# The first hidden units of the MLP move from the last attention step to behind its last values' product

## The chip, the cores and the metric

The kernel runs on one core of one Trainium2 chip. The metric is the device time in microseconds (us) of one execution. The engines are named as the profile names them: PE (TensorE, matrix products), PEld (its weight loads), DVE (VectorE), ACT (ScalarE), POOL (GpSimd) and SP (SyncE, which here only issues transfers). Each engine works through its own list of instructions in order, and the lists meet only at semaphores.

## The reference

Eight sequences of 256 tokens with 512 features are taken through a small non-local attention block (1x1 convolutions, no softmax, batch norm), and then through a transformer block with two cross attentions over the same context (16 heads of 128, one bias key and value added to each head) and an MLP:

```
x = x + attention(layer_norm(x), ctx, weights 1)      # softmax(q k^T / sqrt(128)) v, 16 heads
x = x + attention(layer_norm(x), ctx, weights 2)
h = layer_norm(x)
x = x + gelu(h @ w_fc1 + b_fc1) @ w_fc2 + b_fc2        # 512 -> 2048 -> 512, exact gelu
```

All is float32. The kernel gets that precision by splitting each operand of a product into a high part (rounded to the fp32r format) and the remainder, and by three matrix products in place of one: high by high, high by low, low by high. These three are lines 848, 849 and 850.

## The kernel before

The 2048 rows of x lie in the on-chip memory as 16 tiles of 128 rows, four tiles to a chunk, and there are four chunks (c = 0 to 3). An attention **step** s is one pair of heads for one chunk; there are 64 steps (2 layers x 8 pairs x 4 chunks), numbered 0 to 63. A step has four **items** (two batches x two heads), so the items run from 0 to 255, and the last step, 63, holds items 252 to 255. The work on one item J is:

- `L`, `logits(J)`: PE multiplies queries by keys into the bank `S` (6 matmuls of 258 columns). There is one `S`, so `L` of J+1 waits until ACT has read `S` of J (`exped`).
- DVE takes the minimum of each row (line 1543, `nm`), ACT the exponentials with their sums (line 1225, two of them), DVE the reciprocals of the sums (line 1547), ACT divides by them (line 1233, two).
- `T`, `turn(J)`: PE turns the probabilities (4 small matmuls, line 995) into the bank `T`; ACT copies the high part (line 1243, `PT`), DVE makes the low part (line 1551).
- `P`, `weighted(J)`: PE multiplies by the values into the bank `O` (6 matmuls of 256 columns). ACT reads the high part out (line 1249, `oT`), DVE the low part (line 1558). There is one `O`, so the next `P` waits for that (`o_done`).

What remains goes through a ring of four banks called `U`; a unit takes the bank of the unit four places before it in PE's order and waits until that one has been read out. The units are:

- `q` (s, h): queries of the next step, 12 matmuls, issued in two halves of 6, before and behind a `P`.
- `w` (s, t), t = 0 to 3: output projection of step s for tile t, 6 matmuls, added to x by DVE (line 1535).
- `Z` (n, c, ch), ch = 0 to 3: four small matmuls (line 938) that turn normalised rows. ACT reads them in two dependent instructions (lines 1192 and 1195), DVE in one (line 1515). Norm 2 is the MLP's. Its chunk 1 is turned during step 63, its chunks 2 and 3 behind it.
- `f` (m, i), i = 0 or 1: half of a hidden step of the MLP, 12 matmuls. ACT applies gelu (line 1211, `tmp`) and copies the high part (line 1219), DVE makes the low part `gT` (line 1526, two operands in SBUF).
- `W` (m, t): the second product of the MLP, 6 matmuls, added to x by DVE. There are 32 steps m, chunk m mod 4.

The order of PE is written out by hand: `front_order()`, then `slot_order(s, j)` for the four slots j of each of the 64 steps (one slot an item), then `last_order()`. In a slot, PE does `L` of item J+1, `T` of item J, a first filler, `P` of item J-1 and a second filler; for j = 0 and 2 the fillers are the two halves of a unit `q` of the next step. In the last step there is no next step: the helper `projection` puts there the units `f` (0, 0) and `f` (0, 1), the MLP's first for chunk 0. In slots 1 and 3, and in slots 1 to 3 for `Z`, the fillers are units `w` and `Z`.

ACT and DVE have loops of their own over the same slots. ACT's slot is: queries or hidden (slots 1 and 3), the copy of T (J), the exponentials (J+1), in slots 2 and 3 a `Z` row, `oT` (J-1), the division (J+1), and in slots 1 and 3 one more `Z` row. `hidden(0, j // 2)` stands first in slots 1 and 3 of the last step. DVE's slot has hidden in the same place, between an output and the low part of `PT`. Behind the slots both follow `last_order()`.

`last_order()` starts with P (255), f (1, 0), w (63, 2), w (63, 3), f (1, 1); then Z (2, 2, 0 to 3) mixed with W (0, 0 to 3), f (2, 0), f (2, 1), and Z (2, 3, ...) mixed with W (1, ...); from there on it is regular. DVE does statistics and moments of chunk 3 right behind w (63, 3). POOL splits the MLP's first output weights (`outputs(16)`: a cast at line 644, a subtraction at line 647) once w (63, 3) has been made, then takes a power for chunk 3 once DVE has the moments, then splits the weights `wqs_c` (`queries(17)`) and later adds a bias to the rows. SP's transfers wait for these splits.

Of the kernel before, what the change touches and what calls it, by code (L numbers as in the profile page):

```python
# [38 lines left out]
P = 128  # L39
# [13 lines left out]
STEPS = HBODIES * CHUNKS  # L53
MSTEPS = MBODIES * CHUNKS
ITEMS = 4 * STEPS
# [121 lines left out]
def norm_at(s):  # L177

    for n in range(NORMS):
        c = s - 2 - (n * BODIES * CHUNKS - CHUNKS)  # L180
        if 0 <= c < CHUNKS:
            return n, c
    return None


def projection(s, h, half):
    return ("q", s, h, half) if s < STEPS else ("f", s - STEPS, h, half)


def slot_order(s, j):  # L190

    item = 4 * s + j
    if j in (0, 2):
        first, second = ([projection(s + 1, j // 2, half)] for half in range(2))
    elif j == 1:
        first, second = ([("w", s - 1, t)] if s else [] for t in (2, 3))
    else:
        first, second = ([("w", s, t)] for t in (0, 1))
    rows = [("Z", *norm_at(s), ch) for ch in range(CH)] if norm_at(s) else None
    out = [("L", item + 1)] if item + 1 < ITEMS else []  # L200
    out += [("T", item)] + first
    if rows and j in (1, 3):
        out.append(rows[0 if j == 1 else 3])
    out += [("P", item - 1)] if item else []
    out += second
    if rows and j in (1, 2):
        out.append(rows[j])
    return out


def last_order():

    def f(m, i):
        return [("f", m, i, half) for half in range(2)] if m < MSTEPS else []

    def rows(c):
        return [("Z", LAYERS, c, ch) for ch in range(CH)]

    def mixed(m, c, before):

        out = []
        for t in range(4):
            out += [rows(c)[ch] for ch in before[t]] + [("W", m, t)]
        return out

    out = [("P", ITEMS - 1)] + f(1, 0) + [("w", STEPS - 1, 2), ("w", STEPS - 1, 3)] + f(1, 1)
    out += mixed(0, 2, ((0,), (1,), (2,), (3,))) + f(2, 0) + f(2, 1) + mixed(1, 3, ((), (0, 1), (2,), (3,)))
    for m in range(2, MSTEPS):
        out += f(m + 1, 0) + f(m + 1, 1) + [("W", m, t) for t in range(4)]
    return out  # L230
# [37 lines left out]
def bass_xattn(nc, x_in, ctx_in, thw, thb, pgw, pgb, www, bncol, wa, wk, wv, wb, hcol, vrow,  # L268
               lncol, f1col, orow, out):
    ctx = ExitStack()  # L270
    with ctx:
# [6 lines left out]
        def f(ap):  # L278

            return ap.bitcast(F32)  # L280
# [118 lines left out]
        def bank(*name):  # L399
            return U[:, UNIT[name] % RING, :]  # L400
# [680 lines left out]
        def _(act):  # L1081
# [100 lines left out]
            def rows(n, c, ch):  # L1182
                k = (n * CHUNKS + c) * CH + ch
                act.wait_ge(unit, UNIT["Z", n, c, ch] + 1)
                if k > 1:
                    former = [u for u in UNIT if u[0] == "Z"][k - 2]
                    act.wait_ge(free, FREE[former] + 1)
                else:
                    act.wait_ge(z_x, TILES)
                    act.wait_ge(summed, SUMS)  # L1190
                col = n * CH + ch
                act.activation(hT[c][:, 0, ch, :], bank("Z", n, c, ch), ACT.Identity, bias=lnc[:, 1, col:col + 1],  # L1192
                               scale=lnc[:, 0, col:col + 1]).then_inc(ln_hi, 1)
                act.wait_ge(ln_hi, k + 1)
                act.activation(aff[:, k % 2, :], f(hT[c][:, 0, ch, :]), ACT.Identity, bias=lnn[:, col:col + 1]).then_inc(ln_affine, 1)

            def queries(s, h):
                at_ = 2 * (s // CHUNKS) + h
                act.wait_ge(unit, UNIT["q", s, h] + 1)
                if s and h == 0:  # L1200
                    act.wait_ge(logit, 4 * s - 1)
                elif s:
                    act.wait_ge(logit, 4 * s)
                act.activation(qT[:, 0, h, :], bank("q", s, h), ACT.Identity, bias=hc[:, 0, at_:at_ + 1]).then_inc(hi, 1)

            def hidden(m, i):
                at_ = 2 * (m // CHUNKS) + i
                act.wait_ge(unit, UNIT["f", m, i] + 1)
                if m:
                    act.wait_ge(free, FREE["f", m - 1, i] + 1)  # L1210
                act.activation(tmp[:, i, :], bank("f", m, i), ACT.Gelu, bias=f1c[:, at_:at_ + 1]).then_inc(gelu, 1)  # L1211
                if m > 1 and i == 0:
                    act.wait_ge(unit, UNIT["W", m - 2, 3] + 1)
                elif m == 0 and i == 0:
                    act.wait_ge(logit, ITEMS - 4)
                elif m == 1 and i == 0:
                    act.wait_ge(pv, ITEMS - 4)
                act.wait_ge(gelu, GELU["f", m, i] + 1)
                act.activation(gT[m % 2][:, 0, i, :], tmp[:, i, :], ACT.Copy).then_inc(g_hi, 1)  # L1219

            def exponentials(J):
                r = J % 2
                act.wait_ge(least, J + 1)
                for qt in range(2):
                    ins = act.activation(probs[:, r, qt, 0:257], S[:, qt, 0:257], ACT.Exp, bias=nm[:, r, qt:qt + 1],  # L1225
                                         scale=-1.0, accum_out=sums[:, r, qt:qt + 1])
                ins.then_inc(exped, 1)
# [8 lines left out]
            def turned_hi(J):  # L1236
                act.wait_ge(turned, J + 1)
                if J > 1:
                    act.wait_ge(pv, J - 1)
                else:  # L1240
                    for i in range(4):
                        act.wait_ge(sent[i], 16 * len(KV) // 4)
                act.activation(PT[:, J % 2, 0, :], T[:], ACT.Copy).then_inc(pt_hi, 1)  # L1243
# [35 lines left out]
            for s, j in SLOTS:  # L1279
                J = 4 * s + j  # L1280
                if j % 2 and s + 1 < STEPS:
                    queries(s + 1, j // 2)
                elif j % 2:
                    hidden(0, j // 2)
                turned_hi(J)
                if J + 1 < ITEMS:
                    exponentials(J + 1)
                z_of = norm_at(s)
                if z_of and j > 1:
                    rows(*z_of, j - 1)  # L1290
                if J:
                    weighted_hi(J - 1)
                if J + 1 < ITEMS:
                    divided(J + 1)
                if z_of and j in (1, 3):
                    rows(*z_of, 0 if j == 1 else 3)
# [11 lines left out]
        def _(dve):  # L1308
# [215 lines left out]
            def hidden(m, i):  # L1524
                dve.wait_ge(g_hi, GELU["f", m, i] + 1)
                dve.tensor_tensor(gT[m % 2][:, 1, i, :], tmp[:, i, :], f(gT[m % 2][:, 0, i, :]), ALU.subtract).then_inc(free, 1)  # L1526
# [14 lines left out]
            def least_of(J):  # L1541
                dve.wait_ge(logit, J + 1)
                dve.tensor_reduce(nm[:, J % 2, :], S[:, :, 0:257], AX.X, ALU.min).then_inc(least, 1)  # L1543
# [17 lines left out]
            for k, (what, *a) in enumerate(FRONT):  # L1561
# [10 lines left out]
                elif what == "V":  # L1572
                    r, q, product_of = a
# [23 lines left out]
            for s, j in SLOTS:  # L1597
                J = 4 * s + j
                z_of, z_former, measured = norm_at(s), norm_at(s - 1), norm_at(s + 1) if s else None
                if J + 1 < ITEMS:  # L1600
                    least_of(J + 1)
                if j == 0 and s:
                    if z_former:
                        rows(*z_former, 3)
                    output("w", s - 1, 1)
                elif j == 2:
                    if z_of:
                        rows(*z_of, 0)
                    if s:
                        output("w", s - 1, 3)  # L1610
                if j % 2 and s + 1 < STEPS:
                    queries(s + 1, j // 2)
                elif j % 2:
                    hidden(0, j // 2)
                turned_lo(J)
                if j == 1 and s:
                    output("w", s - 1, 2)
                elif j == 3 and not z_of:
                    output("w", s, 0)
                if J + 1 < ITEMS:  # L1620
                    inverted(J + 1)
                if z_of and j > 1:
                    rows(*z_of, j - 1)
                if J:
                    weighted_lo(J - 1)
                if z_of and j == 3:
                    output("w", s, 0)
                if measured and s > 1:
                    for t in ((0, 1), (2,), (3,), ())[j]:
                        stats_of(s - 1, t)  # L1630
                    if j == 2:
                        moments(*measured)
# [77 lines left out]
```

## Time and profile before

| | |
|---|---|
| median of 3 runs | 2297.21 us (2295.78 to 2297.26) |
| the profiled execution | 2296.15 us |
| its span, first to last instruction | 2294.3 us |
| PE busy | 2271.1 us, 99% of the span |
| DVE busy | 1372.1 us, 60% |
| POOL busy | 1244.9 us, 54% |
| ACT busy | 1168.1 us, 51% |
| mean granted clock of PE | 0.999 |

A profile shows one execution. Its 2294.3 us of span have 1.85 us around them that no engine's instructions fill. PE is busy in nearly every slice of the page; the end of a matmul is modelled, so short idle times are best measured from start to start.

### The profile page before, as it was taken

The numbers are of one execution on the slowest core, as the hardware profiler recorded it, in microseconds if no ns is written. First come the engines' busy times: TensorE is split into PE (matmuls) and PEld (weight loads), VectorE is DVE, ScalarE is ACT, GpSimd is POOL, SyncE is SP. The second block draws the span as 40 slices with busy tenths as digits, with TensorE's granted clock in tenths as the row PEclk, the third lists the DMA queues.
The fourth block names the chain that finished last, engine by engine and source line by source line (L and its number), as shares of the span: only waits on it lengthen the run. The fifth ranks groups of instructions, "written<-read, shape, count | busy, mean of one in ns | idle before, by whom it ended". The sixth has DMA issues, their size and how long they took to land.

```text
span 2294.3 us, 36328 instructions
## 1 busy us (share of the span) xinstructions
PE 2271.1 (99%) x13192; PEld 1987.4 (87%) x13192; DVE 1372.1 (60%) x2381; ACT 1168.1 (51%) x2967; POOL 1244.9 (54%) x983
## 2 busy tenths in 40 slices
PE   8999999999999999999999999999999999999999
PEld 5998987899998888888888888888888888888887
DVE  4676665676654666666666776666666667544333
ACT  4323233323224766666666786666666668322221
POOL 4977772968758675444443786555434456511110
PEclk9999999999999999999999999999999999999999
DMA  4545443454544222222222212222222220100001
GB/s 174 203 157 184 169 164 119 148 194 161 188 160 138 70 79 70 65 74 74 65 70 78 74 56 70 79 79 74 73 67 74 74 65 28 37 23 25 28 1 74
DMA packets 83407, 218.33 MB, mean 95 GB/s; under 512 B 9504, under 2 KB 12064, under 8 KB 83232
## 3 DMA queue, kind: packets, MB, share of 16 engines
q1 hardware_dynamic: 82512, 215.91, 28.1%
q8 instruction: 108, 1.77, 0.3%
q14 instruction: 67, 0.55, 0.1%
q10 hardware_dynamic: 720, 0.10, 0.0%
HBM read 144.41 MB, written 71.57 MB: 94 GB/s over the span
## 4 chain that ended last, share of the span: by engine, by line
PE 76%; ACT 2%; DVE 1%; POOL 1%; issue 0%; ACTq 0%; DVEq 0%
PE U L848 18%; PE U L850 18%; PE U L849 18%; PE T L995 5%; PE S L850 3%; PE S L848 3%; PE S L849 3%; PE O L848 3%; PE O L850 3%; PE O L849 3%; PE U L938 1%; DVE gT L1526 1%; POOL z L766 0%; ACT tmp L1211 0%; ACT hT L1192 0%
## 5 line engine op out<-in xcount | busy, mean ns | idle before, releaser
L1543 DVE TENSOR_REDUCE nm<-S 128x2 f32<-128x514 f32 x256 | 177.5, 693 | 255.9 <-PE S L850 255.8
L1535 DVE TENSOR_TENSOR x<-x,U 128x512 f32<-128x512 f32 x384 | 260.1, 680 | 37.3 <-PE U L850 35.4
L1243 ACT ACTIVATE PT<-T 128x512 fp32r<-128x512 f32 x256 | 152.5, 596 | 173.8 <-PE T L995 173.2
L1225 ACT ACTIVATE probs<-S,nm 128x257 f32<-128x257 f32 x512 | 237.6, 476 | 2.6 <-DVE nm L1543 2.3
L1233 ACT ACTIVATE probs<-probs,rs 128x256 f32<-128x256 f32 x512 | 230.1, 499 | 1.3 <-DVE rs L1547 1.3
L848 PE MATMUL U<-wos,oT 128*128 128x512 f32 x512 | 213.0, 416 | 0.2 <-DVE gT L1526 0.2
L1558 DVE SCALAR_TENSOR_TENSOR oT<-O,hc,oT 128x256 fp32r<-128x256 f32 x256 | 123.7, 483 | 143.0 <-ACT oT L1249 142.7
L745 POOL CAST vb<-vb 128x1024 fp32r<-128x1024 f32 x64 | 66.6, 1040 | 255.6 <-DMA vb<-vd 255.6
L850 PE MATMUL U<-wos,oT 128*128 128x512 f32 x512 | 201.7, 394 | 0.0
L849 PE MATMUL U<-wos,oT 128*128 128x512 f32 x512 | 200.8, 392 | 0.0
L1249 ACT ACTIVATE oT<-O,hc 128x256 fp32r<-128x256 f32 x256 | 121.0, 473 | 127.7 <-PE O L850 127.6
L1551 DVE TENSOR_TENSOR PT<-T,PT 128x512 fp32r<-128x512 f32 x256 | 174.8, 683 | 0.0
L1211 ACT ACTIVATE tmp<-U,f1c 128x512 f32<-128x512 f32 x64 | 44.0, 688 | 245.7 <-PE U L850 245.7
L739 POOL TENSOR_TENSOR kb<-kb 128x1032 fp32r<-128x1032 f32 x64 | 155.5, 2430 | 5.2
L1526 DVE TENSOR_TENSOR gT<-tmp,gT 128x512 fp32r<-128x512 f32 x64 | 58.0, 907 | 164.9 <-ACT gT L1219 164.9
L848 PE MATMUL U<-hT,wqs 128*128 128x512 f32 x384 | 155.7, 405 | 0.8 <-DVE hT L1515 0.8
L747 POOL TENSOR_TENSOR vb<-vb 128x1024 fp32r<-128x1024 f32 x64 | 153.3, 2395 | 5.1
L995 PE MATMUL T<-ident,probs 128*128 128x128 f32 x1024 | 154.0, 273 | 1.3 <-ACT probs L1233 1.2
L850 PE MATMUL U<-hT,wqs 128*128 128x512 f32 x384 | 150.7, 392 | 0.0
L849 PE MATMUL U<-hT,wqs 128*128 128x512 f32 x384 | 150.1, 391 | 0.0
L848 PE MATMUL S<-kb,qT 128*128 128x258 f32 x512 | 146.4, 286 | 0.3 <-ACT probs L1225 0.3
L850 PE MATMUL S<-kb,qT 128*128 128x258 f32 x512 | 145.2, 284 | 0.0
(247 smaller groups left out, 7225.7 us busy)
## 6 DMA issues: line engine op xcount, KB each, us to landing
kd<-stage SPq DMA_DIRECT2D x128, 258.0 KB, 2.5
kb<-kd SPq DMA_DIRECT2D x64, 516.0 KB, 3.4
vd<-stage SPq DMA_DIRECT2D x128, 256.0 KB, 2.1
vb<-vd SPq DMA_DIRECT2D x64, 512.0 KB, 3.8
raw<-wk SPq DMA_DIRECT2D x32, 512.0 KB, 5.3
rawv<-wv SPq DMA_DIRECT2D x28, 512.0 KB, 4.4
raw<-wa SPq DMA_DIRECT2D x24, 512.0 KB, 4.6
raw<-wb SPq DMA_DIRECT2D x24, 512.0 KB, 5.0
```

The lines of the kernel that those rows point to most:

```text
L739: pool.tensor_tensor(lo_part_of, f(lo_part_of), f(hi_part_of), ALU.subtract).then_inc(k_lo, 1)
L747: pool.tensor_tensor(lo_part_of, f(lo_part_of), f(hi_part_of), ALU.subtract).then_inc(v_lo, 1)
L848: pe.matmul(o, lhs[0], rhs[0], start=start, stop=False)
L849: pe.matmul(o, lhs[0], rhs[1], start=False, stop=False)
L850: return pe.matmul(o, lhs[1], rhs[0], start=False, stop=stop)
L995: mm = pe.transpose(T[:, at_:at_ + P], probs[:, J % 2, qt, tt * P:tt * P + P], ident[:])
L1225: ins = act.activation(probs[:, r, qt, 0:257], S[:, qt, 0:257], ACT.Exp, bias=nm[:, r, qt:qt + 1], scale=-1.0, accum_out=sums[:, r, qt:qt ...
L1233: ins = act.activation(probs[:, r, qt, 0:256], probs[:, r, qt, 0:256], ACT.Copy, scale=rs[:, r, qt:qt + 1])
L1243: act.activation(PT[:, J % 2, 0, :], T[:], ACT.Copy).then_inc(pt_hi, 1)
L1535: dve.tensor_tensor(x[:, tile, :], x[:, tile, :], bank(what, s, t), ALU.add).then_inc(free, 1)
L1543: dve.tensor_reduce(nm[:, J % 2, :], S[:, :, 0:257], AX.X, ALU.min).then_inc(least, 1)
L1551: dve.tensor_tensor(PT[:, J % 2, 1, :], T[:], f(PT[:, J % 2, 0, :]), ALU.subtract).then_inc(pt, 1)
```

## The change

The units f (0, 0) and f (0, 1) are taken out of slots 0 and 2 of the last attention step and put behind P (255), the attention's last product with the values. ACT and DVE lose their `hidden` calls in slots 1 and 3 of that step and do them where `last_order()` has the units. No unit is added or dropped, and its size and its number of instructions stay as they were. The banks of the ring are given out anew by the new order.

```diff
-def projection(s, h, half):
-    return ("q", s, h, half) if s < STEPS else ("f", s - STEPS, h, half)
-
 def slot_order(s, j):
     item = 4 * s + j
     if j in (0, 2):
-        first, second = ([projection(s + 1, j // 2, half)] for half in range(2))
+        first, second = ([("q", s + 1, j // 2, half)] if s + 1 < STEPS else [] for half in range(2))
...
 def last_order():
-    out = [("P", ITEMS - 1)] + f(1, 0) + [("w", STEPS - 1, 2), ("w", STEPS - 1, 3)] + f(1, 1)
+    out = [("P", ITEMS - 1)] + f(0, 0) + [("w", STEPS - 1, 2), ("w", STEPS - 1, 3)] + f(0, 1) + f(1, 0) + f(1, 1)
...
 # ACT's slots
                 if j % 2 and s + 1 < STEPS:
                     queries(s + 1, j // 2)
-                elif j % 2:
-                    hidden(0, j // 2)
                 turned_hi(J)
...
 # DVE's slots
                 if j % 2 and s + 1 < STEPS:
                     queries(s + 1, j // 2)
-                elif j % 2:
-                    hidden(0, j // 2)
                 turned_lo(J)
```

## Rows read from the trace of the kernel before

**Rows 1.** The page, part 1: engine, busy us, share of the span, instructions.

```profile
PE 2271.1 (99%) x13192; PEld 1987.4 (87%) x13192; DVE 1372.1 (60%) x2381; ACT 1168.1 (51%) x2967; POOL 1244.9 (54%) x983
```

**Rows 2.** Timeline of PE, last attention step: start, us, instruction, [idle before <-releaser].

```profile
1912.56 0.62 PE L995 MATMUL T<-ident,probs 128*128 128x128 f32 x4
...
1916.46 0.28 PE L848 MATMUL S<-kb,qT 128*128 128x258 f32 x1
...
1917.18 0.60 PE L995 MATMUL T<-ident,probs 128*128 128x128 f32 x4
1917.54 0.48 PE L848 MATMUL U<-wos,oT 128*128 128x512 f32 x1
...
1919.01 0.60 PE L938 MATMUL U<-ident,z 128*128 128x128 f32 x4
...
1920.15 0.40 PE L848 MATMUL U<-wos,oT 128*128 128x512 f32 x1
...
1929.04 0.66 PE L995 MATMUL T<-ident,probs 128*128 128x128 f32 x4 [0.87 <-ACT probs L1233]
...
1934.89 0.35 PE L848 MATMUL O<-PT,vb 128*128 128x256 f32 x1 [0.79 <-DVE oT L1558]
...
1941.13 0.39 PE L848 MATMUL U<-hT,wqs 128*128 128x512 f32 x1
...
1943.86 0.60 PE L938 MATMUL U<-ident,z 128*128 128x128 f32 x4
1944.93 0.50 PE L848 MATMUL U<-wos,gT 128*128 128x512 f32 x1 [0.48 <-POOL wos L647]
```

**Rows 3.** Timeline of ACT, same stretch.

```profile
1915.07 0.21 ACT L1225 ACTIVATION_READ_ACCUMULATOR probs<-S,nm 128x1 f32 x1
...
1915.97 0.91 ACT L1233 ACTIVATE probs<-probs,rs 128x256 f32<-128x256 f32 x2 [0.21 <-DVE rs L1547]
1916.90 1.28 ACT L1211 ACT_TABLE_LOAD   x1
...
1924.92 0.58 ACT L1243 ACTIVATE PT<-T 128x512 fp32r<-128x512 f32 x1
1925.39 0.47 ACT L1225 ACTIVATE probs<-S,nm 128x257 f32<-128x257 f32 x1
...
1926.29 0.79 ACT L1192 ACTIVATE hT<-U,lnc 128x512 fp32r<-128x512 f32 x1
...
1927.74 0.45 ACT L1249 ACTIVATE oT<-O,hc 128x256 fp32r<-128x256 f32 x1
1928.09 0.90 ACT L1233 ACTIVATE probs<-probs,rs 128x256 f32<-128x256 f32 x2
...
1935.87 0.48 ACT L1249 ACTIVATE oT<-O,hc 128x256 fp32r<-128x256 f32 x1 [0.52 <-PE O L850]
```

**Rows 4.** Timeline of ACT at the start: the kernel's first table load.

```profile
13.01 1.28 ACT L1114 ACT_TABLE_LOAD   x1 [13.01 <-PE U L884]
```

**Rows 5.** Timeline of DVE, last attention step and behind it.

```profile
1934.27 0.47 DVE L1558 SCALAR_TENSOR_TENSOR oT<-O,hc,oT 128x256 fp32r<-128x256 f32 x1
...
1945.44 0.69 DVE L1526 TENSOR_TENSOR gT<-tmp,gT 128x512 fp32r<-128x512 f32 x1 [0.53 <-ACT gT L1219]
```

**Rows 6.** Timeline of DVE, a later unit.

```profile
2016.60 2.72 DVE L1526 TENSOR_TENSOR gT<-tmp,gT 128x512 fp32r<-128x512 f32 x1 [1.97 <-ACT gT L1219]
```

**Rows 7.** Timeline of POOL.

```profile
1941.37 1.04 POOL L644 CAST wos<-raw 128x1024 fp32r<-128x1024 f32 x1 [0.94 <-PE U L850]
...
1944.99 1.03 POOL L753 TENSOR_TENSOR rstd<-vpe,minus_half 128x4 f32<-128x4 f32 x1
...
2016.37 2.40 POOL L647 TENSOR_TENSOR wqs_c<-raw,wqs_c 128x1024 fp32r<-128x1024 f32 x1
```

**Rows 8.** Timeline of PE in the first attention step.

```profile
738.47 1.05 PE L938 MATMUL U<-ident,z 128*128 128x128 f32 x4 [1.56 <-POOL z L766]
```

**Rows 9.** Stretches: from:to, length, busy (instructions) per engine, PEclk, DMA share, GB/s.

```profile
738.60:742.00 3.40, 3.40 (x17) 3.40 (x18) 0.54 (x2) 1.16 (x3) 3.31 (x3) 0.50 0.05 22
```

## The prediction

> **What bounds the kernel now.** The page's busy times come first: PE is busy for 99% of the span, so the time is PE's work plus its pauses [rows 1]. The change leaves PE's work alone, so I read PE's timeline only where its order changes and note, from start to start, each place where an instruction begins later than the one before it needs. The lists of ACT and DVE in the same stretch tell what set those starts. The waits on record are short: for the divided probabilities of item 255 (0.87 us idle, T at 1929.04), for `oT` at P (255) (0.79) and for the MLP's first output weights at W (0, 0) (0.48) [rows 2]. So in the last step PE is only just the bound; behind it stands ACT's chain from T to T: copy of T, two exponentials, a row of Z, `oT`, two divisions [rows 3].
>
> **Strides of PE** (start to start, nothing waited for) [rows 2]: L 0.72 (1916.46 to 1917.18), T 0.36 (to 1917.54), w 1.47 behind a T (to 1919.01), Z and P together 1.14 (to 1920.15), which I split into 0.36 and 0.78. A whole unit f takes 2.73 (1941.13 to 1943.86), and a w that is not behind a T half of that, 1.37.
>
> **What is taken out of the step.** PE loses 2 x 2.73 = 5.46 us. ACT loses two gelus with their copies and two changes of table, to gelu in slot 1 and back to exponentials in the same slot; the third load, before the second gelu, becomes the single load that the kernel needs in any case. A load holds ACT for 1.28 us [rows 3].
>
> **The step anew, item by item.** All up to T (252) at 1912.56 stays.
> - P (251) follows at 1912.92 and ends its 0.78 at 1913.70. L (254) needs `S`, read out at 1915.07 + 0.21 = 1915.28 [rows 3]; nothing changes there, so L (254) starts at 1915.35: a pause of 1.65 us where f (0, 0) was.
> - T (253) needs the division, 1915.97 + 0.91 = 1916.88 [rows 3], so it starts at 1916.94, 0.24 before its old time; pause 0.87.
> - From there PE sets the pace: T 0.36, w 1.47, Z 0.36, so P (252) at 1919.13; with its 0.78, w 1.37 and Z 0.36, L (255) is at 1921.64 and T (254), 0.8 behind it, at 1922.45. The division for T (254) is ready before: `oT` comes 0.98 us behind the start of P (252) (1934.89 to 1935.87 [rows 2, 3]), at 1920.11, and 0.35 and 0.95 behind that (1927.74 to 1928.09 to T at 1929.04 [rows 2, 3]) it is 1921.41.
> - T (255) is where the cover is gone. From T (254) at 1922.45: the copy of T starts 0.64 later (0.36 of issue and the 0.28 that a small matmul lasts), the exponentials 0.47 later (1924.92 to 1925.39), then 0.90 (to 1926.29), the row of Z 1.45 (to 1927.74), `oT` 0.35, division and release 0.95 [rows 3]. Sum 4.76, so T (255) at 1927.2. PE has only P (253) and one Z to do until then, and is free at 1922.45 + 0.36 + 0.78 + 0.36 = 1923.95: a pause of 3.26 us. Before it started at 1929.04, so the step wins 1.8 there.
> - Then T 0.36, w (63, 0) 1.47, Z 0.36, P (254) at 1929.4 with its 0.78, w (63, 1) 1.4, and P (255) at 1931.6. Its other condition, DVE's `oT` of item 254: ACT at 1929.4 + 0.98 = 1930.4, DVE 0.5 later (estimate, from the length of ACT's part), 0.62 from DVE's start to PE's (1934.27 to 1934.89 [rows 2, 5]) = 1931.5. It fits by 0.1.
>
> P (255) goes from 1934.89 to 1931.6: 3.3 earlier.
>
> **What is added behind it.** PE gets the 5.46 us back. The wait for POOL's weights goes away: Z started at 1943.86 and W (0, 0) could have at 1944.22, but did at 1944.93: 0.71 [rows 2]. POOL starts that split 0.24 us behind w (63, 3) (PE's next unit starts 1941.13, the cast 1941.37) [rows 2, 7]. Three units f now stand between, 8.2 us in place of 2.73, and hide its 3.5 us; if they did not, the old 0.71 is the most that could come back. The queues: SP is moved past nothing; ring banks are given out to readers that are done by then. f (0, 0) runs from 0 to 2.73 (zero is the end of P (255)), w (63, 3) ends at 5.48, f (0, 1) at 8.2, f (1, 0) at 10.9, f (1, 1) at 13.7. The load of the gelu table stands behind its wait for PE, as the first load of the kernel did, which came at 13.01 with PE as the releaser [rows 4], so f (0, 0)'s low part on DVE comes at 2.73 + 1.58 + 1.29 = 5.6 (1.58 is 1943.86 to 1945.44 [rows 2, 5]). Its bank is wanted at 8.2: hidden. But behind it in DVE's list are the sums of w (63, 2) and (63, 3), the statistics and the moments, for which POOL waits before it splits the next weights. That split now meets the low part of f (1, 1), ready at 13.7 + 1.58 = 15.25. DVE's `gT` and POOL's subtraction don't run together: one took 2.72 us in place of 0.69, ending 0.55 behind POOL's 2.40 [rows 5 to 7]. I get POOL's subtraction ending between 15.1 and 16.1 (moments done at 10.5 or 11.5, the spread for whether the low part of f (0, 0) meets the cast or not; power 1.03 and cast 1.04 [rows 7], subtraction 2.4, and the gaps between), so `gT` is done at 15.95 to 16.65, while W (0, 1) wants that bank at 13.7 + 0.36 + 1.47 + 0.36 = 15.9. Cost 0.1 to 0.8; I take 0.4. If the split met it whole, 2.0 (2.72 less 0.69); if not at all, 0.
>
> Sum of these: -3.3 + 5.46 - 0.71 + 0.4 = **+1.9 us**.
>
> **The clock.** When PE stops, more than the stop can be lost. In the first attention step, behind a wait of 1.56 us [rows 8], the granted clock stood at 0.50 (1.2 of 2.4 GHz) for 3.40 us although PE was busy through all of it [rows 9]. Work of 1.7 us took 3.4: such a fall costs up to 1.7 us, and 0 if it fell wholly into the pause. The new pause before T (255) is 3.26 us, twice as long, with only one P and one Z ahead of it. I take one fall and 1.5 us, since part of the low stretch may lie in the pause. The pauses before L (254) and T (253), 1.65 and 0.87 us with 0.7 of work between, could bring another. They too are near the row in length, but shorter each than what surrounds T (255); the long waits of before, at 0.87 and 0.79, brought none (mean clock 0.999).
> The Trainium skill's page "TensorE: Matmul & The Clock Gate", section "HAM oscillation", asks for no long idle gap between bursts of matmuls, and would let a wait as short as that of rows 8 pass. The row goes against it, so I don't take the rule's side; by it the clock might stay up, and the time be that of rival 2.
> On the load of a table the Trainium skill's page "ScalarE: Activation LUTs", section "What ACT_TABLE_LOAD costs", gives some 2.66 us for every switch, with a drain. The trace has 1.28 and the next instruction right behind; by the page the one load left would come 1.4 us later to DVE and could make the 0.4 above 1.8, so the sum +3.3.
>
> So 1.9 + 1.5 = **+3.4 us**. On the profiled execution: 2296.15 + 3.4 = 2299.6. The median stands 1.06 above that execution: 2297.21 + 3.4 = **2300.6 us**.
>
> **The rivals.** What this kernel's runs can tell from no change is about 0.2%, 4.6 us: below 2292.6 is faster, above 2301.8 slower.
> 1. *Slower: two falls of the clock.* Place: the pauses before L (254) and T (253). The work up to T (254), 4.8 us, is PE's own pace, so a fall there delays T (254) and all behind it. It decides if the low stretch covers over 1.2 us of that work. Price 1.5 to 1.7 more: 3.4 + 1.6 = +5.0, 2302.2. For: 2.5 us of pause within 3.7 us. Against: it is broken in two.
> 2. *No fall.* The pauses cost only themselves: +1.9, 2299.1. For: the mean clock of 0.999. Against: rows 8 and 9.
> 3. *The cover was not worth its place: no loss, or a gain.* If ACT's chain in slot 2 runs shorter than my sum, for instance because the row of Z slips behind the division, T (255) comes 1.45 us earlier, and with less pause also without a fall: 1.9 - 1.45 = +0.4, and with the smaller cost at W (0, 1) 0.0: 2297.2. Against: ACT's list is fixed and has the row first. Floor: even with T (255) unblocked, -3.26 + 1.9 = -1.4: 2295.8.
> 4. *It does not do what it says:* the units keep their number and size, and behind P (255) there is nothing that could hide them; I see no form of this.
>
> **Chances.** One fall 0.40, two falls 0.28, no fall 0.20, no loss 0.10, other 0.02. The likeliest gives 2300.6. The range takes from rival 2 and its lower part to rival 1 with its bound: low 1.9 less 1.9 (a tail of 0 and a chain shorter by a row), 2297.2; high 5.0 plus 0.9 for the split meeting `gT` more fully, 2303.1. All but rival 1 with its like lie within 0.2%: faster 0.03, within 0.62, slower 0.35 (two falls at 0.28, and one fall with a tail at its upper bound).
>
> **What would show it.** Right: PE waits for `probs` before L (254), T (253) and most before T (255), 3 us; no table load for exponentials at the end, one for gelu; PEclk at 0.50 for a few us right at or behind T (255); no wait for POOL at W (0, 0); a short wait for `gT` at W (0, 1). Wrong: T (255) within 1.5 us of its predecessor, a clock of 1.00 throughout, or a wait over 1 us at W (0, 1). Behind W (1, 3) the two traces should run in parallel at a constant distance.

## The result, and the profile after

| | before | after |
|---|---|---|
| median | 2296.91 us (21 runs, 2294.78 to 2297.79) | 2299.69 us (21 runs, 2297.19 to 2301.6) |
| ratio after to before | | 1.0013, 95% interval 1.0007 to 1.0019 |
| span of the profiled execution | 2294.3 us | 2299.8 us |

The change costs 2.8 us, 0.13%. The forecast was 2300.6, +3.4, within 0.2% at a chance of 0.62, with a range of 2297.2 to 2303.1. (The profiled execution after is the slowest of its 21, that of before is below its median; so the two spans are 5.5 apart, and I compare stretches, not spans.)

PE's work is the same 13192 matmuls [rows 1], and its busy time 1.0 us more. The page, part 1, of the kernel after:

```profile
PE 2272.1 (99%) x13192; PEld 1987.1 (86%) x13192; DVE 1376.1 (60%) x2381; ACT 1166.6 (51%) x2965; POOL 1244.9 (54%) x983
```

The timeline of PE in the last attention step, after (start, us, instruction, idle before and releaser). The lines answer to those of [rows 2]; line numbers of PE and ACT are 4 lower:

```profile
1914.50 0.62 PE L991 MATMUL T<-ident,probs 128*128 128x128 f32 x4
...
1917.29 0.39 PE L844 MATMUL S<-kb,qT 128*128 128x258 f32 x1 [1.45 <-ACT probs L1221]
...
1918.88 0.66 PE L991 MATMUL T<-ident,probs 128*128 128x128 f32 x4 [0.61 <-ACT probs L1229]
...
1924.45 0.60 PE L991 MATMUL T<-ident,probs 128*128 128x128 f32 x4
...
1925.59 0.60 PE L934 MATMUL U<-ident,z 128*128 128x128 f32 x4
1929.23 0.66 PE L991 MATMUL T<-ident,probs 128*128 128x128 f32 x4 [3.04 <-ACT probs L1229]
...
1931.60 1.05 PE L934 MATMUL U<-ident,z 128*128 128x128 f32 x4
1932.31 0.56 PE L844 MATMUL O<-PT,vb 128*128 128x256 f32 x1
...
1935.24 0.28 PE L844 MATMUL O<-PT,vb 128*128 128x256 f32 x1
...
1949.98 0.48 PE L844 MATMUL U<-wos,gT 128*128 128x512 f32 x1
...
1951.96 0.50 PE L844 MATMUL U<-wos,gT 128*128 128x512 f32 x1
```

In order: T (252), L (254), T (253), T (254), Z, T (255), then Z, P (254), P (255), W (0, 0), W (0, 1). Each entry is the first product of its unit. Three things are to be seen. There are new waits for `probs`, 1.45, 0.61 and 3.04 us. Z at 1931.60 lasts 1.05 us in place of 0.60 and the next product is 0.71 behind it in place of 0.36: half speed. And W (0, 0) waits for nobody, where it waited for POOL's weights.

Here are the granted clock and busy times of the stretch of the pause, of the stretch that followed and of the one behind it (from:to, length, busy us (instructions) of PE, PEld, DVE, ACT, POOL, then PEclk):

```profile
1925.95:1929.23 3.28, 0.24 (x3) 0.00 (x2) 2.49 (x7) 3.20 (x9) 0.00 (x0) 1.00 0.00 0
1930.60:1934.00 3.40, 3.40 (x14) 2.99 (x14) 1.40 (x2) 1.35 (x3) 2.03 (x2) 0.50 0.00 0
1934.00:1938.00 4.00, 4.00 (x21) 3.36 (x21) 2.82 (x5) 3.60 (x5) 4.00 (x3) 1.00 0.02 4
```

So that executions can be compared, I count from T (252), up to which both orders are the same. In us behind T (252):

| kernel | T (254) | T (255) | P (255) | W (0, 0) | W (0, 1) | falls of the clock in this stretch |
|---|---|---|---|---|---|---|
| before | 11.08 | 16.48 | 22.33 | 32.37 | 34.23 | none |
| after | 9.95 | 14.73 | 20.74 | 35.48 | 37.46 | one, 3.4 us |
| after, second trace | 9.96 | 14.74 | 21.98 | 36.72 | 38.70 | one, 6.8 us |
| stand-in work in slot 2 | 9.96 | 14.75 | 19.16 | 33.88 | 35.86 | none |
| stand-in work in both slots | 9.96 | 14.74 | 19.17 | 33.90 | 35.88 | none |
| unit left in slot 2 | 9.95 | 14.74 | 20.65 | 32.69 | 35.92 | none |
| unit left in slot 0 | 11.10 | 16.51 | 22.41 | 34.43 | 37.65 | one, 3.4 us |
| before, no gelu in step 0 | 10.18 | 14.97 | 19.39 | 29.42 | 31.27 | none |
| row behind the division | 9.95 | 13.76 | 18.78 | 33.56 | 35.98 | none |
| unit in slot 2, POOL later | 9.95 | 14.74 | 20.64 | 32.71 | 34.69 | none |

The table gives 37.46 - 34.23 = 3.23 us between before and after. From W (0, 1) to the end of the span it is 347.5 us before and 347.8 after. The rest of the 5.5 lies ahead of T (252) (1912.56 and 1914.50), where nothing was changed: over the ten traces T (252) came between 1911.6 and 1914.5. The 0.3 behind W (0, 1) is mostly at W (0, 2), which comes 2.08 us behind W (0, 1) after and 1.83 before.

ACT after, in slot 2 and behind the slots: the copy of T (254), the last division, the one load of the gelu table, the first gelu.

```profile
1925.09 0.60 ACT L1239 ACTIVATE PT<-T 128x512 fp32r<-128x512 f32 x1 [0.28 <-PE T L991]
...
1928.28 0.90 ACT L1229 ACTIVATE probs<-probs,rs 128x256 f32<-128x256 f32 x2
...
1936.65 1.28 ACT L1207 ACT_TABLE_LOAD   x1
1938.92 0.69 ACT L1207 ACTIVATE tmp<-U,f1c 128x512 f32<-128x512 f32 x1 [0.99 <-PE U L846]
```

From 1925.09 to 1928.28 is ACT's chain that holds T (255). The load comes at 1936.65, right behind `oT` of item 255, and f (0, 0)'s gelu at 1938.92 still waits 0.99 us for PE: the load did not wait for PE's unit.

DVE's and POOL's lines behind the slots, after:

```profile
1940.36 0.69 DVE L1520 TENSOR_TENSOR gT<-tmp,gT 128x512 fp32r<-128x512 f32 x1 [2.71 <-ACT gT L1215]
...
1948.55 1.84 DVE L1520 TENSOR_TENSOR gT<-tmp,gT 128x512 fp32r<-128x512 f32 x1 [2.09 <-ACT gT L1215]
1951.21 0.69 DVE L1520 TENSOR_TENSOR gT<-tmp,gT 128x512 fp32r<-128x512 f32 x1 [0.82 <-ACT gT L1215]
```

```profile
1941.70 1.05 POOL L640 CAST wos<-raw 128x1024 fp32r<-128x1024 f32 x1 [0.67 <-PE U L846]
...
1947.44 2.40 POOL L643 TENSOR_TENSOR wqs_c<-raw,wqs_c 128x1024 fp32r<-128x1024 f32 x1
```

The low part of f (1, 0), at 1948.55, took 1.84 us: POOL's subtraction ran from 1947.44 to 1949.84, and DVE ended 0.55 behind it, the distance of [rows 6, 7]. The low part of f (1, 1), at 1951.21, took 0.69.

### The profile page after: what moved, and what is told of

It is laid out like the page before. It is cut to its first block, busy times and chain, and to the rows that moved or that the text cites. A ratio compares the mean times of both kernels' runs of the same rounds, so it can differ in the third digit from the quotient of the medians.

```text
span 2299.8 us, 36326 instructions
## 1 busy us (share of the span) xinstructions
PE 2272.1 (99%) x13192; PEld 1987.1 (86%) x13192; DVE 1376.1 (60%) x2381; ACT 1166.6 (51%) x2965; POOL 1244.9 (54%) x983
## 4 chain that ended last, share of the span: by engine, by line
PE 76%; DVE 1%; ACT 1%; issue 0%; POOL 0%; DVEq 0%; ACTq 0%
PE U L844 18%; PE U L846 18%; PE U L845 18%; PE T L991 5%; PE S L846 3%; PE S L844 3%; PE S L845 3%; PE O L844 3%; PE O L846 3%; PE O L845 3%; PE U L934 1%; DVE gT L1520 1%; POOL z L762 0%; ACT hT L1188 0%; ACT probs L1221 0%
```

## The experiments

"Ratio" is to the kernel before run beside them. In the first four it had a median of 2297.0 us, in the second four of 2296.52, each over 33 runs.

**The changed kernel again.** No edit.

> The changed kernel once more, as the yardstick for the runs beside it. From T (252) to W (0, 1) it took 37.46 us where the kernel before took 34.23. Theory (pauses of PE plus one fall of its clock): +1.6 us over the kernel before in an execution without a fall, 1.5 to 1.7 more for each fall, so a median of +2.5 to +3.3. Rival (the fall costs nothing, the pauses are all): executions at a mean clock of 1.000 are no faster than those at 0.999.

Measured: 2300.55 us (11 runs), ratio 1.0016 (1.0007 to 1.0025), so +3.6, a little over the +2.5 to +3.3. The two executions at a mean clock of 1.000 took 2299.19 and 2299.33, the six at 0.999 2298.98 to 2301.09 with a median of 2300.4, the three at 0.998 2301.3 to 2302.35. In the 21 runs of the result it was the same: six at 1.000 with a median of 2298.2, fifteen at 0.999 or 0.998 with a median of 2300.4. The rival is wrong: executions with a lower clock are slower as a group. The new trace shows a fall of double length (the columns as above, the second stretch the one behind it):

```profile
1928.20:1935.06 6.86, 6.30 (x22) 5.48 (x23) 3.02 (x10) 2.95 (x7) 2.69 (x2) 0.51 0.00 1
1935.06:1939.00 3.94, 3.94 (x21) 3.33 (x20) 2.82 (x5) 3.18 (x5) 3.94 (x3) 1.00 0.02 4
```

It began inside the pause, at about 1928.05 (the stretch shown starts a little later), and went on for 6.8 us. P (255) came 2.8 us later than without a fall (21.98 against 19.16).

**Stand-in work in slot 2.** The pause is filled and nothing else is changed:

```diff
 def slot_order(s, j):
...
+    if s == STEPS - 1 and j == 2:
+        out.append(("N",))
...
+            def stand_in():
+                o = take("w", STEPS - 1, 0)
+                for ch in range(CH):
+                    mm = product(o, parts(query_weights(HBODIES), ch, slice(0, P)), parts(hT[0], ch), ch == 0, ch == CH - 1)
```

> The changed kernel, with 12 matmuls that nobody reads in PE's list behind the Z of slot 2, into the bank that w (63, 0) overwrites. Its 2.73 us lie in the pause before T (255). Theory: T (255) stays at 14.7 us behind T (252), as ACT's chain sets it, the clock stays at 1.00, P (255) comes at 19.1 in place of 20.7, and the time is 1.6 us below the changed kernel's, still about 1.7 above the kernel before. Rival 1 (the fall comes from the earlier pauses before L (254) and T (253), or costs nothing): no change against the changed kernel. Rival 2 (PE is the bound there after all): T (255) comes up to 2.7 later and the time rises.

Measured: 2298.2 us (11 runs), ratio 1.0010 (1.0001 to 1.0019). T (255) at 14.75, P (255) at 19.16, clock at 1.00. PE's T (255) and P (255), and the clock over the filled pause and the 8 us behind it:

```profile
1927.84 0.66 PE L998 MATMUL T<-ident,probs 128*128 128x128 f32 x4 [0.17 <-ACT probs L1238]
...
1932.25 0.31 PE L846 MATMUL O<-PT,vb 128*128 128x256 f32 x1
```

```profile
1924.40:1927.84 3.44, 3.27 (x16) 2.34 (x15) 2.65 (x7) 3.35 (x9) 0.00 (x0) 1.00 0.00 0
1928.00:1936.00 8.00, 8.00 (x46) 6.82 (x46) 5.12 (x13) 5.71 (x9) 6.60 (x4) 1.00 0.01 3
```

The wait at T (255) is 0.17 in place of 3.04 us, though 2.73 us of matmuls were added, and T (255) stands where it did. So PE did not set it. P (255) is 1.58 us earlier than in the changed kernel's first trace; T (255) stands at the same place in both and the order behind it is the same, so what differs is the clock. The median is 2.35 below the changed kernel's beside it, where 1.6 was expected; falls as long as the second trace's would make up the rest. The eight executions at 1.000 took 2297.64 to 2298.93. Three at 0.999 took 2301.6 to 2302.1, 4 us more, which is more than the one fall priced here; where their clock fell no trace shows.

**Stand-in work in both slots.** As above, and 6 matmuls into the bank of w (62, 2) behind P (251):

```diff
+    if s == STEPS - 1 and j in (0, 2):
+        out.append(("N", j))
```

> The changed kernel with unread matmuls in both pauses: 12 behind slot 2 as in the earlier run and 6 behind P (251) in slot 0. Theory: positions as with the one stand-in, W (0, 1) at 35.9 us behind T (252); the executions at a mean clock of 0.999, 3 of 11 with one stand-in and some 4 us slower, become as rare as in the kernel before if the slot-0 pauses cause them, and stay 3 of 11 or so if they come from elsewhere (the first attention step has its own waits).

Measured: 2298.33 us (11 runs), ratio 1.0009 (1.0001 to 1.0018). Positions as with one stand-in, within 0.02. All eleven executions stood at 1.000, against three at 0.999 with slot 0 empty. That would fit falls behind slot 0's pauses, but it does not show them: 0 of 11 against 3 of 11 proves little, and the kernel before, which has no pause in slot 0, stood at 0.999 in 19 of its 66 executions. One more sign points at slot 0 without settling it. In the kernel before, the executions at 0.999 have medians 0.5 and 1.5 us above those at 1.000; with slot 0 empty and slot 2 filled they lie 3.9 us (stand-in work in slot 2) and 3.0 us (unit left in slot 2) above, but with POOL later the two such executions lie only 0.5 and 2.4 above. No trace caught one of them, so this stays open. What remains with no fall is the price of the new order itself: 35.88 - 34.23 = 1.65 us by the traces, 1.8 by the medians.

**A unit left in slot 2.**

```diff
-... [("q", s + 1, j // 2, half)] if s + 1 < STEPS else [] ...
+... [("q", s + 1, j // 2, half)] if s + 1 < STEPS else [("f", 0, 0, half)] if j == 2 else [] ...
-    out = [("P", ITEMS - 1)] + f(0, 0) + [w (63, 2), w (63, 3)] + f(0, 1) + f(1, 0) + f(1, 1)
+    out = [("P", ITEMS - 1)] + f(0, 1) + [w (63, 2), w (63, 3)] + f(1, 0) + f(1, 1)
...
+                elif j == 3:
+                    hidden(0, 0)          # ACT and DVE
```

> Half of the change: slot 0 is left empty, slot 2 keeps a unit, f (0, 0), with its gelu in slot 3; f (0, 1) goes behind P (255). The two changes of table in slot 1 are gone as in the changed kernel. Theory: T (255) at 14.7 us behind T (252) as in the changed kernel, no fall of the clock, P (255) about 20.5 behind T (252) since the table load and the gelu stand before the copy of T (before: 22.33), and with 2.73 of a unit added and 0.7 of the wait for the weights gone: +0.3 us against the kernel before, some 2.5 below the changed one. Rival (the time is lost to the empty slot 0 as much as to the empty slot 2): +1.5 or more.

Measured: 2298.37 us (11 runs), ratio 1.0007 (0.9999 to 1.0016), so +1.4 by the medians where +0.3 was expected. T (255) at 14.74 and P (255) at 20.65 came as expected, with no fall in the trace. The miss is at W (0, 1), 3.23 behind W (0, 0) in place of 1.86: 1.37 us, which is all of the miss in the trace (35.92 - 34.23 = 1.69, less 1.37 is the 0.3 expected). The median (+1.4) nearly fits the rival (+1.5 or more), the place does not: T (254) and T (255) come no later than in the kernel before. Five of the eleven executions stood at 0.999; their median is 2300.3, that of the six at 1.000 2297.3. DVE's low part of f (1, 1), then POOL's subtraction:

```profile
1945.51 1.94 DVE L1522 TENSOR_TENSOR gT<-tmp,gT 128x512 fp32r<-128x512 f32 x1 [1.97 <-ACT gT L1215]
```

```profile
1944.51 2.39 POOL L643 TENSOR_TENSOR wqs_c<-raw,wqs_c 128x1024 fp32r<-128x1024 f32 x1
```

**The same, with POOL later.**

```diff
                 elif E == HBODIES + 1:
-                    pool.wait_ge(logit, ITEMS)
+                    pool.wait_ge(free, FREE["f", 1, 1] + 1)
```

> The kernel with a unit left in slot 2, in which W (0, 1) came 1.37 us late since the low part of f (1, 1) stood behind POOL's subtraction (1.94 us in place of 0.69). Here POOL waits for that low part before it splits the weights `wqs_c`. Theory: `gT` of f (1, 1) takes 0.69, W (0, 1) comes 34.5 us behind T (252) in place of 35.68, 1.1 to 1.2 us gained, level with the kernel before (34.23) without a fall of the clock. Rival (the release is late because ACT's gelu is, the lock matters little): under 0.4 gained.

Measured: 2298.05 us (11 runs), ratio 1.0006 (0.9997 to 1.0014). The low part of f (1, 1), and POOL's cast behind it:

```profile
1947.49 0.69 DVE L1522 TENSOR_TENSOR gT<-tmp,gT 128x512 fp32r<-128x512 f32 x1 [1.97 <-ACT gT L1215]
```

```profile
1948.25 1.04 POOL L640 CAST wqs_c<-raw 128x1024 fp32r<-128x1024 f32 x1 [2.89 <-DVE gT L1522]
```

It takes 0.69 us in place of 1.94, and W (0, 1) follows W (0, 0) by 1.98 in place of 3.23: 1.25 us of wait gone. W (0, 1) is at 34.69, 1.23 earlier than in the run above and still 0.46 behind the kernel before. (The 35.68 in the expectation is 35.92 when counted from the first matmul of T (252).) The medians of the two (+1.4 and +1.5 over the kernel before beside them) don't show the gain that the traces do, and over the executions at 1.000 alone they go the other way (+0.6 and +2.1). Runs of one kernel lie 4 us apart, and 11 of them can't tell it: the gain is shown in this stretch of one trace each, not in the time.

**A unit left in slot 0.** The same edit with `j == 0` in the order and `j == 1` for `hidden`.

> The other half: slot 0 keeps f (0, 0) with its gelu and both changes of table in slot 1; slot 2 is empty and f (0, 1) stands behind P (255). Theory: T (254) as before (11.1 us behind T (252)), then ACT's chain of 4.76 with PE idle for 3.2 of it, T (255) at 15.8, a fall of the clock as in the changed kernel, P (255) at 20.3 without and 21.9 with it; in sum +0.2 us against the kernel before without a fall, +1.8 with one. Rival (the pause needs the empty slot 0 as well before the clock falls): no fall, +0.2.

Measured: 2299.32 us (11 runs), ratio 1.0012 (1.0004 to 1.0021), +2.3. T (254) and T (255) in its trace:

```profile
1924.87 0.66 PE L991 MATMUL T<-ident,probs 128*128 128x128 f32 x4 [0.18 <-ACT probs L1229]
...
1930.28 1.11 PE L991 MATMUL T<-ident,probs 128*128 128x128 f32 x4 [3.60 <-ACT probs L1229]
```

The pause is there with slot 0 filled, 3.60 us idle, and the clock stood at 0.50 from about 1930.1 to 1933.5: T (255) takes 1.11 us for 0.66. All eleven executions stood at 0.999. The rival is wrong: the empty slot 2 is enough. The expected position was missed, though: T (255) came at 16.51 and not at 15.8, hardly later than in the kernel before (16.48). The expectation took the chain of 4.76 us from T (254) on, but with the changes of table kept in slot 1, ACT is behind when T (254) runs: it comes late to the divisions, goes through a row of Z without idle time and starts the copy of T (254) 1.28 us behind T (254) (in the kernel before 1923.64 to 1924.92 [rows 3], here 1924.87 to 1926.15) and not 0.64. P (255) was 0.5 later than expected, and W (0, 1) waits 1.15 us for `gT`, as in the kernel with a unit left in slot 2. By the traces that makes +3.4 in place of +1.8, by the medians +2.3.

**The kernel before, without gelu in step 0.** This leaves gelu out for f (0, 0) and f (0, 1).

```diff
-                act.activation(tmp[:, i, :], bank("f", m, i), ACT.Gelu, ...
+                act.activation(tmp[:, i, :], bank("f", m, i), ACT.Gelu if m else ACT.Identity, ...
```

> The kernel before, with identity in place of gelu in f (0, 0) and f (0, 1), so that gelu is left out for step 0 of the MLP and the first table load comes behind P (255). It prices what the table loads cost in the old order. Theory (ACT's chain is the bound in the last step): T (254) at 10.1 us behind T (252) in place of 11.1, T (255) at 14.8 in place of 16.5, P (255) at 19.4 in place of 22.3; the wait for POOL's weights stays; -2.9 us against the kernel before. Rival (the loads hide behind PE's work): under 1 us.

Measured: 2293.58 us (11 runs), ratio 0.9988 (0.9979 to 0.9997), -2.9. T (254), T (255) and W (0, 0):

```profile
1923.80 0.60 PE L995 MATMUL T<-ident,probs 128*128 128x128 f32 x4
...
1928.59 0.66 PE L995 MATMUL T<-ident,probs 128*128 128x128 f32 x4 [0.30 <-ACT probs L1233]
...
1943.04 0.50 PE L848 MATMUL U<-wos,gT 128*128 128x512 f32 x1 [0.48 <-POOL wos L647]
```

Every position is within 0.2 us of the expectation. ACT still does an activation in gelu's place (0.67 us in place of 0.69), so what is gone from the step is the loads: in the old order the two table loads in slot 1 and the one in slot 3 cost 2.96 us (34.23 - 31.27), of 3 x 1.28 = 3.84 us. They were not hidden. The last wait, for POOL's weights, stays at 0.48.

**The row of Z behind the division.** In the changed kernel, slot 2 of step 63 only:

```diff
-                if z_of and j > 1:
+                if z_of and j > 1 and not late:      # late: s == STEPS - 1 and j == 2
                     rows(*z_of, j - 1)
...
+                if late:                             # behind divided (ACT), weighted_lo (DVE)
+                    rows(*z_of, 1)
```

> The changed kernel, with ACT's and DVE's row of Z in slot 2 put behind the division and behind `oT`. This is the order of my third rival. Theory: T (255) at 13.3 us behind T (252) in place of 14.7, pause 1.8 in place of 3.3, P (255) at 17.7 (19.2 without a fall before), so 1.5 us below the changed kernel without a fall, and fewer falls: a median near the kernel before's, +0.2 us. Rival (the row only moves ACT's work to slot 3, and P (255) stays): T (255) earlier but P (255) at 19.1.

Measured: 2299.16 us (11 runs), ratio 1.0012 (1.0003 to 1.0021). PE's T (255) and P (255), and ACT's division, the row behind it and the copy of T (255):

```profile
1927.63 0.66 PE L991 MATMUL T<-ident,probs 128*128 128x128 f32 x4 [2.07 <-ACT probs L1229]
...
1932.65 0.36 PE L844 MATMUL O<-PT,vb 128*128 128x256 f32 x1 [0.45 <-DVE oT L1555]
```

```profile
1926.67 0.91 ACT L1229 ACTIVATE probs<-probs,rs 128x256 f32<-128x256 f32 x2 [0.34 <-DVE rs L1544]
1927.48 0.76 ACT L1188 ACTIVATE hT<-U,lnc 128x512 fp32r<-128x512 f32 x1
...
1928.90 0.58 ACT L1239 ACTIVATE PT<-T 128x512 fp32r<-128x512 f32 x1
```

T (255) came 1.0 us earlier in place of 1.4 (the division waits 0.34 us for DVE's reciprocal, which the row used to cover), but P (255) only 0.4 (18.78 against 19.16): the row now holds up the copy of T (255), and P (255) waits 0.45 for `oT`. Even the 0.4 is lost by W (0, 1), at 35.98 against the stand-in's 35.86: it comes 2.42 behind W (0, 0) in place of 1.98, since the low part of f (1, 1) now meets POOL's subtraction.

```profile
1948.66 1.13 DVE L1523 TENSOR_TENSOR gT<-tmp,gT 128x512 fp32r<-128x512 f32 x1 [1.67 <-ACT gT L1215]
```

```profile
1946.53 2.73 POOL L643 TENSOR_TENSOR wqs_c<-raw,wqs_c 128x1024 fp32r<-128x1024 f32 x1
```

My expectation was wrong: P (255) lies nearer the rival's 19.1 than my 17.7, and the median is +2.6 in place of +0.2. A pause of 2.07 us brought no fall in this trace; four of the eleven executions stood at 0.999, fewer than with the full pause (24 of 32 below 1.000).

## Why the prediction was right

**The step anew: right.** T (255) was put 14.6 us behind T (252) and came at 14.73; the pause was put at 3.26 from start to start and was 3.28 (the Z at 1925.59 and its 0.36, to 1929.23). Without a fall P (255) comes at 19.16, so it wins 3.17 where I had 3.3. That ACT sets T (255) is shown by the stand-in: 2.73 us of matmuls in the pause moved it by 0.02.

**What is added behind: right.** From P (255) to W (0, 0) it is 10.04 us before and 14.74 after: 4.70 more, against 5.46 - 0.71 = 4.75. The wait for POOL's weights is gone, as three units f hide it.

**The tail: the size was right by luck, the working was not.** I had the table load behind its wait for PE, from the kernel's first load. Behind the slots it came at once, 2.3 us ahead of the gelu, in time in which ACT had nothing to do. So the low part of f (0, 0) was ready 4.4 us behind P (255)'s end, not 5.6, DVE's statistics ended earlier, POOL's subtraction ended at 13.9 us and not at 15.1 to 16.1, and it met the low part of f (1, 0), whose bank is not wanted so soon, rather than f (1, 1)'s. W (0, 1) lost 0.12 (1.98 less 1.86) in place of 0.4. Even that 0.12 is not the meeting's: the low part of f (1, 1) took its 0.69 us undisturbed, and the same 0.12 is left when POOL is held back. So the meeting that the term priced did not happen at this bank. The mechanism is real elsewhere: with one unit f fewer behind P (255) it cost 1.37 and 1.36 us in the two half-changes, and went to 0.12 when POOL was held back.

**The clock: right, with a wider spread than was priced.** I priced one fall at 1.5; the first trace has one that cost 1.58, the second a stretch of 6.8 us that cost 2.8. The wait of 1.57 us in the first attention step brought a fall in three of ten traces, so short gaps are not safe either, and the new pause of 3.04 us idle brought one in both traces of the changed kernel. The Trainium skill's page "TensorE: Matmul & The Clock Gate", section "HAM oscillation", warns only of idle gaps longer than these; the traces do not agree with it. By the pause in both traces and by 24 of 32 executions below 1.000, rival 2 is not what happens in most executions.

**The sum.** 5.46 - 3.17 - 0.71 + 0.12 + 1.58 = 3.28, against 3.23 between the two traces. Over many executions the forecast of +3.4 is 0.6 above the measured +2.8 and 0.2 below the +3.6 of the second set. The terms without the clock make 1.7 (1.9 forecast), and executions without a fall are about a quarter: 8 of 32 at 1.000, against 23 of 33 for the kernel before beside the first four.

**The rivals.** Two separate falls, the first at L (254): neither trace has it. The one long fall of the second trace comes near its price (38.70 - 34.23 = +4.5 against +5.0) by another way. Two figures given for this rival don't come out of the prediction's own positions: the two pauses lie within 3.2 us, not 3.7, and the work from T (253) to T (254) is 5.5, not 4.8; neither enters the forecast. Rival 3 named the row of Z, and the experiment shows that moving it gives 0.4 us at P (255) and nothing at W (0, 1). No reason was left for a gain: to pay, the change would have had to win on ACT's chain more than the 4.75 us that it adds behind P (255). Set the two halves of that side by side: with only the table loads gone, and PE's fillers and ACT's activations kept, P (255) came at 19.39; with those gone too, at 19.16 (the stand-in's, without a fall). So 5.46 us of PE's work, with ACT's four instructions for it, had cost 0.23 us where it was, and of the 3.17 us that the change won, 2.94 came from the table loads that left the step. Behind P (255) that work costs its full length.

**A better version?** The half-change with POOL held back comes nearest: W (0, 1) at 34.69 against 34.23, no fall in its trace, ratio 1.0006 with an interval that holds 1. The half-change without that hold is not told apart from it by the medians (1.0007). None of those tried beats the kernel before.

## What to carry to other kernels

A filler on the busiest engine is worth its own length as long as another engine's chain runs under it; taking it out gains only what its companions cost on that chain (here 3.2 us for 5.5, nearly all of it three table loads). Price the pause as well by what it does to TensorE's clock: here the new order cost 1.65 us by itself and one fall behind its pause 1.58 more, in most executions. And if a unit moves, follow its low-priority companions too: where a VectorE instruction with two SBUF operands meets a GpSimd one is set by the order of everything ahead of both.

## What the runs showed of the hardware that was not expected

The same wait on the same instruction does not always bring the clock down. PE's first wait for POOL's normalised rows, in the second trace of the changed kernel, in its first, and in the run with both stand-ins:

```profile
740.01 0.97 PE L934 MATMUL U<-ident,z 128*128 128x128 f32 x4 [1.57 <-POOL z L762]
```

```profile
741.32 0.66 PE L934 MATMUL U<-ident,z 128*128 128x128 f32 x4 [1.57 <-POOL z L762]
```

```profile
738.69 0.66 PE L936 MATMUL U<-ident,z 128*128 128x128 f32 x4 [1.57 <-POOL z L764]
```

The wait is 1.57 us in all three. In the first the transposes behind it take 0.97 us, in the others 0.66. The clock fell at this place in three of ten traces: in the kernel before [rows 8, 9], the second trace after, and the one without gelu.

A fall can last twice as long as the next. It was 3.4 us in the first trace after and 6.8 in the second, behind a pause of the same length and with the same work following it; in the second it began 0.7 us ahead of the pause's end, in the first 1.4 us behind it (T (255) at 1929.23, the clock at 0.50 from 1930.6). Why one was double stays open.

A table load need not wait for the data of the instruction that it serves. The one behind the slots ran at once behind `oT`, while the kernel's first [rows 4] came with PE's first result. What makes the difference was not tried.
